# A decoder layer on one core: the front taken in pairs of tiles, half of the tokens first, with three loads issued from ScalarE's queue

## The chip, the core and the metric

One core of a Trainium2 chip runs the whole program. The time is the device time in microseconds (us) of one execution; lower is better. Three runs of the kernel before are at hand, and one further execution was recorded by the hardware profiler.

## The reference, cut to what matters

The layer takes x, 8 batches of 128 tokens with 512 features. The change is in its first stage, the mamba block up to the scores:

```python
h = rmsnorm(x, ln1_w)                 # x * rsqrt(mean(x * x) + eps) * ln1_w
zxbcdt = h @ w_in.T                   # 512 -> 1284: z, xs, Bs, Cs, dt
xBC = silu(conv4(xs | Bs | Cs) + conv_b)      # causal, 4 taps along the tokens, 768 channels
dt = softplus(dt + dt_bias)
cs = cumsum(dt * -exp(A_log))
att = (Cs @ Bs.T) * exp(cs_q - cs_k)          # for each batch and head
...
```

Behind it come the rest of the mamba block, a gated MLP, an attention over ctx and an expert layer, each with its normalisation. None of that is touched.

## The kernel before, in words

All products are made in three passes. An operand is split into a high part (rounded to the fp32r type) and a low part (the rest), and `three_pass` (L336) issues high x low, high x high and low x high; L338, L339 and L340 are these three matmuls. So each weight and each activation has to be split before TensorE may use it: ScalarE writes the high part by a copy (`hi_part` L653, `hi_of_hT` L685), and GpSimd (`lo_part` L281, the weights) or VectorE (`low1` L940, the activations) subtracts it for the low part.

**Tiles.** A tile is one batch of 128 tokens: x comes as eight tiles x0 to x7, and two halves (hf 0 and 1) of four tiles each make 512 columns. For each tile: ScalarE sums the squares (L665) and makes the reciprocal root by Ln and Exp (`rms`, L671 and L673), for two tiles at a time (`norm1(t0, t1)`); VectorE multiplies by it and by the LN1 row `ln1r`, which a DMA has broadcast to all 128 partitions (L931); TensorE turns the tile by four transposes (`turn_h`, L349) into bank 0 or 1; ScalarE and VectorE split what stands there (L687, L937).

**Weights.** `w_in` comes in six chunks of 128 x 1024 (0.5 MB), each of two blocks m of 128 output columns. A chunk is loaded into one of three raw buffers (`load_chunk`, L219), split by ScalarE (L657) and GpSimd (L283) into one of two ring buffers, and used by the projections of its two blocks. GpSimd counts `w_lo` when a chunk is ready; SyncE waits on it before it loads the next into the raw buffer, and ScalarE waits on `ip_done` before it writes the ring (`ring_hi`, L659).

**Projection.** Product n (`in_proj`, L352) is block m and half hf by `IN_ORDER` (L56): before, (0,0), (1,0), (0,1), (1,1), then m = 2 to 10 with both halves each. A whole product is 12 matmuls of 512 columns; in the front a product is also taken in two parts of 256 columns (two tiles). Products go round six banks (`IN_BANK`, L330), and a bank is free again when VectorE (`ip_used`) or ScalarE (`z_done`) has read it. Block 0 gives dt (`softplus_in`, L950; `softplus`, L689), blocks 1 to 6 go through the convolution (`conv_last_tap` L697 on ScalarE, three `conv_taps` L986 on VectorE, `conv_silu` L705 on ScalarE, with two buffers `acc`), blocks 7 to 10 are z. `time_steps` (L964) makes the cumulative sums, and `scores_of(0)` (L374) is issued after product 17; it needs those sums and the convolved values.

**Order.** Each engine has one instruction stream, written out by hand, and waits only on semaphores. TensorE's front is at L443 to L469: matmuls of zeros (`keep_warm`, L438) stand between the transposes and the first products. ScalarE's is at L742 to L765, VectorE's at L943 to L1003, GpSimd's at L285 to L295. SyncE issues all loads (L216 to L241), in this order: x0, x1, the LN1 row, x2, x3, chunk 0, eleven constants, x4 to x7, chunks 1 and 2, then the later chunks as they are waited for.

## Time and profile before

| what | us |
|---|---|
| median of 3 runs (lowest to highest) | 433.39 (433.07 to 433.83) |
| span of the profiled execution | 432.9 |
| that execution's own time, outside the span | not recorded; the median stands 0.5 above the span |
| TensorE busy in the span | 417.5 |
| VectorE / ScalarE / GpSimd busy | 211.8 / 161.4 / 67.6 |

The span runs from the first to the last instruction of the core. In the rows below, PE is TensorE's matmuls, PEld its weight loads, DVE VectorE, ACT ScalarE, POOL GpSimd and SP SyncE; a q behind a name is the engine's sequencer, which issues DMAs. A line number is that of the instruction in the kernel, which may be a helper's. Starts and ends of matmuls are modelled, so two that follow each other overlap in the rows: their pace is the distance of their starts.

### The profile page before, as it was taken

Reading aid. Unit: us, or ns where it says so; the run is one execution under the profiler, and the core shown is the slowest. Engines: PE = TensorE matmul, PEld = TensorE weight load, DVE = VectorE, ACT = ScalarE, POOL = GpSimd, SP = SyncE. Lnnn points to the kernel's source line nnn. Section 1 sums busy time; section 2 is a strip of 40 time slices with the busy share of each in tenths; the row PEclk is TensorE's granted clock in tenths of the full one; section 3 lists DMA queues with packets and bytes.
Section 4 is the critical chain, followed back from the end, with each engine's and each line's share of the span. In section 5 each row is a group of like instructions: output and inputs, shape, how many; then the busy total and the mean of one; then the engine's idle time right before and its main releaser. Section 6 shows DMA issues by size and latency. Waiting matters only on the chain.

```text
span 432.9 us, 5328 instructions
## 1 busy us (share of the span) xinstructions
PE 417.5 (96%) x1966; PEld 331.7 (77%) x1966; DVE 211.8 (49%) x392; ACT 161.4 (37%) x327; POOL 67.6 (16%) x51
## 2 busy tenths in 40 slices
PE   7999999999999999999999999999999999999984
PEld 2788887766667888888888888888787887887763
DVE  1586996135774431212122222254366576576566
ACT  5636655555653521212121212243232232241221
POOL 2412222344292110101010202020000000000000
PEclk9799999999999999999999999999999999999998
DMA  7610210020020021212121212111101201201001
GB/s 218 246 50 2 91 55 28 22 97 2 0 98 2 2 97 48 97 48 97 48 97 48 97 48 97 48 50 48 48 2 48 74 24 49 73 24 51 24 0 73
DMA packets 10256, 25.67 MB, mean 59 GB/s; under 512 B 1696, under 2 KB 1824, under 8 KB 10240
## 3 DMA queue, kind: packets, MB, share of 16 engines
q1 hardware_dynamic: 9088, 23.36, 16.1%
q10 hardware_dynamic: 1152, 2.10, 1.3%
q8 instruction: 10, 0.16, 0.2%
q14 instruction: 6, 0.05, 0.0%
HBM read 23.36 MB, written 2.10 MB: 59 GB/s over the span
## 4 chain that ended last, share of the span: by engine, by line
PE 88%; DVE 5%; ACT 3%; issue 1%; DMA 1%; SPq 0%; ACTq 0%; DVEq 0%
PE bank L338 25%; PE bank L339 25%; PE bank L340 25%; PE bank L394 2%; PE bank L382 2%; PE bank L546 2%; PE bank L535 1%; DMA rows<-x 1%; PE bank L557 1%; PE bank L403 1%; DVE tmp L1087 1%; PE bank L424 1%; PE bank L349 1%; PE bank L527 1%; PE bank L441 1%
## 5 line engine op out<-in xcount | busy, mean ns | idle before, releaser
L338 PE MATMUL bank<-cols,ringS 128*128 128x512 f32 (+1 forms) x328 | 126.6, 386 | 1.4 <-DVE cols L937 1.3
L340 PE MATMUL bank<-cols,ringS 128*128 128x512 f32 (+1 forms) x328 | 124.5, 380 | 0.0
L339 PE MATMUL bank<-cols,ringS 128*128 128x512 f32 (+1 forms) x328 | 124.5, 380 | 0.0
L338 PEld LDWEIGHTS bank<-cols,ringS 128*128 128x128 f32 x328 | 62.1, 189 | 15.0 <-issue 2.9
L339 PEld LDWEIGHTS bank<-cols,ringS 128*128 128x128 f32 x328 | 62.1, 189 | 11.8 <-issue 0.5
L340 PEld LDWEIGHTS bank<-cols,ringS 128*128 128x128 f32 x328 | 61.9, 189 | 11.6
L1054 DVE TENSOR_TENSOR big<-tmp,bank 128x512 f32 (+1 forms) x28 | 19.3, 688 | 102.2 <-ACT tmp L798 102.2
L338 PE MATMUL bank<-wdS,cols 128*128 128x512 f32 x144 | 61.4, 427 | 0.0
L340 PE MATMUL bank<-wdS,cols 128*128 128x512 f32 x144 | 56.4, 392 | 0.0
L339 PE MATMUL bank<-wdS,cols 128*128 128x512 f32 x144 | 56.2, 390 | 0.0
L798 ACT ACTIVATE tmp<-bank 128x512 f32<-128x512 f32 x28 | 16.8, 598 | 105.6 <-PE bank L340 105.6
L324 POOL TENSOR_TENSOR wdS<-raw,wdS 128x1024 f32 x7 | 16.8, 2394 | 122.2 <-ACT wdS L804 122.2
L338 PEld LDWEIGHTS bank<-wdS,cols 128*128 128x128 f32 x144 | 27.2, 189 | 7.7 <-issue 1.9
L339 PEld LDWEIGHTS bank<-wdS,cols 128*128 128x128 f32 x144 | 27.1, 189 | 6.6 <-issue 1.9
L340 PEld LDWEIGHTS bank<-wdS,cols 128*128 128x128 f32 x144 | 27.0, 188 | 6.0
L986 DVE SCALAR_TENSOR_TENSOR tmp<-bank,cw,tmp 128x508 f32<-128x508 f32 (+2 forms) x36 | 26.7, 742 | 5.5 <-ACT tmp L702 3.4
L283 POOL TENSOR_TENSOR ringS<-raw,ringS 128x1024 fp32r<-128x1024 f32 x8 | 20.2, 2533 | 52.8 <-ACT ringS L657 52.8
L837 ACT ACTIVATE small<-small 128x1 f32<-128x1 f32 x24 | 7.1, 294 | 50.7 <-DVE small L1089 50.7
L1059 DVE TENSOR_TENSOR ringS<-raw,ringS 128x1024 fp32r<-128x1024 f32 x14 | 17.2, 1227 | 2.3 <-ACT ringS L804 0.5
L1087 DVE BATCH_NORM_STATS2 tmp<-tmp 128x6 f32<-128x512 f32 x24 | 16.7, 694 | 0.8
L1009 DVE SCALAR_TENSOR_TENSOR big<-bank,xb,big 128x128 f32<-128x128 f32 x32 | 9.0, 342 | 16.5 <-ACT big L726 16.5
L937 DVE TENSOR_TENSOR cols<-bank,cols 128x512 fp32r<-128x512 f32 x16 | 10.9, 687 | 12.5 <-ACT cols L687 7.8
(134 smaller groups left out, 513.2 us busy)
## 6 DMA issues: line engine op xcount, KB each, us to landing
raw<-wstream SPq DMA_DIRECT2D x31, 512.0 KB, 3.2
rows<-x SPq DMA_DIRECT2D x8, 256.0 KB, 4.6
big<-ctxT SPq DMA_DIRECT2D x8, 256.0 KB, 2.6
big<-ctx SPq DMA_DIRECT2D x8, 256.0 KB, 2.9
out<-tmp ACTq DMA_DIRECT2D x8, 256.0 KB, 2.0
big<-ln_w SPq DMA_DIRECT2D x2, 256.0 KB, 5.4
big<-lora_b SPq DMA_DIRECT2D x3, 64.0 KB
ga<-gate_lora SPq DMA_DIRECT2D x1, 72.0 KB
```

The costliest lines, as they stand in the source:

```text
L283: pool.tensor_tensor(dst, raw[:, raw_slot(n), :], hi.bitcast(F32), ALU.subtract).then_inc(w_lo, 1)
L324: pool.tensor_tensor(wdS_t[:, bass.ds(j * CH + NM * D, CH)], raw[:, 0, :], wdS_t[:, bass.ds(j * CH, CH)].bitcast(F32), ALU.subtract).then_ ...
L338: pe.matmul(ps, a_hi, b_lo, start=first, stop=False)
L339: pe.matmul(ps, a_hi, b_hi, start=False, stop=False)
L340: return pe.matmul(ps, a_lo, b_hi, start=False, stop=last)
L798: act.activation(hn[:, par, :], bank[4 * par + 2 * hf][:, :], ACT.Silu).then_inc(sg_ok, 1)
L937: v.tensor_tensor(token_cols(t, 1), blocks(src), token_cols(t, 0).bitcast(F32), ALU.subtract).then_inc(done, 1)
L986: v.scalar_tensor_tensor(out=dst[:, :, s:L], in0=src[:, :, 0:L - s], scalar=cw[:, m, 3 - s:4 - s], in1=dst[:, :, s:L], op0=ALU.mult, op1=A ...
L1009: v.scalar_tensor_tensor(out=dec[:, b % 2, h, :], in0=bank[6][:, bass.ts(h, L)], scalar=xb[:, b % 2, P + H + h:P + H + h + 1], in1=dec[:, ...
L1054: v.tensor_tensor(dst, blocks(hn[:, par, :]), blocks(bank[4 * par + 2 * hf + 1][:, :]), ALU.mult) \
L1059: v.tensor_tensor(ringS[:, par, 1, :], raw[:, par + 1, :], ringS[:, par, 0, :].bitcast(F32), ALU.subtract).then_inc(ring_lo, 1)
L1087: v.bn_stats(stats[:, k, :], u).then_inc(ln_st[i], 1)
```

## The change

The front goes by pairs of tiles, and in the order of the products all four blocks of chunks 0 and 1 come first for half 0, then for half 1. Chunk 0 is loaded second, and it is split in two pieces with semaphores of their own (`w0_hi`, `w0_lo`). ScalarE's queue issues the LN1 row (one partition, 2 KB), x1 and chunk 1. The LN1 row is spread to 128 partitions by a matmul with ones into bank 7, and VectorE reads it there. The constants are two groups, four for the taps (`taps_in`) and seven others. `keep_warm` has 18 matmuls of zeros in place of 26, into bank 6. On ScalarE, softplus of half 1 moves behind the third convolution product. The core of the diff:

```diff
-IN_ORDER = ((0, 0), (1, 0), (0, 1), (1, 1)) + tuple((m, hf) for m in range(2, N_IN) for hf in range(2))
-N_CONST = 11
+IN_ORDER = tuple((m, hf) for hf in range(2) for m in range(4)) \
+    + tuple((m, hf) for m in range(4, N_IN) for hf in range(2))
+CONV_ORDER = tuple((m, hf) for m, hf in IN_ORDER if 1 <= m <= N_CONV)
+N_TAPS = 4
+N_CONST = 7
+def last_of_chunk(n):
+    return max(i for i, (m, hf) in enumerate(IN_ORDER) if m // 2 == n)
...
-        ln1r = big[:, 13312:13824]
+        ln1row = acc[0:1, 0, :]
+        LN1_BANK = 7
```

SyncE's loads:

```diff
-            for t in range(2):
-                sp.dma_start(rows[:, t, :], x[t]).then_inc(x_in[t], 16)
-            sp.dma_start(ln1r, ln1_w.partition_broadcast(P)).then_inc(ln1_in, 16)
-            for t in range(2, HB):
-                sp.dma_start(rows[:, t, :], x[t]).then_inc(x_in[t], 16)
+            load_rows(0, 1)
             load_chunk(0)
-            for dst, src in ((alog[:, :], a_log), (dtb[:, :], dt_bias), (cw[:, :, :], conv_w),
-                             (cb[:, :], conv_b), (dsk[:, :], d_skip.partition_broadcast(P)),
+            load_rows(2, HB)
+            load_rows(HB, HB + 2)
+            for dst, src in ((alog[:, :], a_log), (dtb[:, :], dt_bias), (cw[:, :, :], conv_w), (cb[:, :], conv_b)):
+                sp.dma_start(dst, src).then_inc(taps_in, 16)
+            load_rows(HB + 2, B)
+            load_chunk(2)
+            for dst, src in ((dsk[:, :], d_skip.partition_broadcast(P)),
                              (ln2r, ln2_w.partition_broadcast(P)), (ga[:, :, :], gate_lora),
                              *((lb[bass.ts(i, E * RANK), :], lora_b) for i in range(3)),
                              (eb[:, :], expert_bias.partition_broadcast(P))):
                 sp.dma_start(dst, src).then_inc(const_in, 16)
-            for t in range(HB, B):
-                sp.dma_start(rows[:, t, :], x[t]).then_inc(x_in[t], 16)
-            load_chunk(1)
-            load_chunk(2)
```

GpSimd's low parts of the weights:

```diff
-            for n in range(IN_CHUNKS):
+            for q in range(2):
+                q_ = bass.ts(q, D)
+                pool.wait_ge(w0_hi, q + 1)
+                pool.tensor_tensor(ringS[:, 0, 1, q_], raw[:, raw_slot(0), q_], ringS[:, 0, 0, q_].bitcast(F32),
+                                   ALU.subtract).then_inc(w0_lo, 1)
+            pool.wait_ge(w0_lo, 2)
+            pool.sem_inc(w_lo, 1)
+            for n in range(1, IN_CHUNKS):
                 lo_part(n, ringS[:, n % 2, 1, :], ringS[:, n % 2, 0, :])
-                if n == 0:
+                if n == 2:
```

TensorE's waits and its order up to n = 4:

```diff
-                pe.wait_ge(w_lo, m // 2 + 1)
+                if m < 2:
+                    pe.wait_ge(w0_lo, m + 1)
+                else:
+                    pe.wait_ge(w_lo, m // 2 + 1)
...
-            zeros = (7, idle[:, 0, 0:P], idle)
-            WARM = (4, 4, 2, 2, 2)
+            zeros = (6, idle[:, 0, 0:P], idle)
             pe.wait_ge(idle_ok, 1)
-            keep_warm(12, *zeros)
-            pe.wait_ge(pool_setup, 8)
+            keep_warm(10, *zeros)
+            pe.wait_ge(vec_setup, 1)
+            pe.wait_ge(ln1_in, 16)
+            pe.matmul(bank[LN1_BANK][:, :], ones[0:1, :], ln1row, start=True, stop=True).then_inc(ln1_ps, 1)
+            pe.wait_ge(pool_setup, 3)
             turn_h(0)
             turn_h(1)
-            keep_warm(WARM[0], *zeros)
+            keep_warm(4, *zeros)
+            in_proj(0, 2, 0)
+            in_proj(1, 2, 0)
+            keep_warm(2, *zeros)
             turn_h(2)
-            keep_warm(WARM[1], *zeros)
-            in_proj(0, 2, 0)
             turn_h(3)
-            in_proj(1, 2, 0)
-            keep_warm(WARM[2], *zeros)
+            keep_warm(2, *zeros)
             in_proj(0, 2, 1)
+            in_proj(1, 2, 1)
             turn_h(4)
-            in_proj(1, 2, 1)
             turn_h(5)
-            keep_warm(WARM[3], *zeros)
+            in_proj(2)
+            in_proj(3, 2, 0)
             turn_h(6)
-            in_proj(2, 2, 0)
             turn_h(7)
-            in_proj(3, 2, 0)
-            keep_warm(WARM[4], *zeros)
-            in_proj(2, 2, 1)
             in_proj(3, 2, 1)
```

ScalarE:

```diff
             def ring_hi(n):
                 if n >= 2:
-                    act.wait_ge(ip_done, 4 * (n - 1))
+                    act.wait_ge(ip_done, last_of_chunk(n - 2) + 1)
...
+            act.dma_start(ln1row, ln1_w.partition_broadcast(1)).then_inc(ln1_in, 16)
+            act.dma_start(rows[:, 1, :], x[1]).then_inc(x_in[1], 16)
+            act.dma_start(raw[:, raw_slot(1), :], wstream[1]).then_inc(raw_in[raw_slot(1)], 16)
             act.preload_act_table_set(LN_EXP)
             norm1(0, 2)
+            act.wait_ge(raw_in[raw_slot(0)], 16)
+            for q in range(2):
+                q_ = bass.ts(q, D)
+                act.activation(ringS[:, 0, 0, q_], raw[:, raw_slot(0), q_], ACT.Copy).then_inc(w0_hi, 1)
+            act.sem_inc(w_hi, 1)
+            hi_of_hT(0)
+            hi_of_hT(1)
             norm1(2, HB)
-            hi_of_hT(0)
-            hi_part(0, ringS[:, 0, 0, :])
-            hi_of_hT(1)
+            ring_hi(1)
             hi_of_hT(2)
+            hi_of_hT(3)
             norm1(HB, HB + 2)
-            hi_of_hT(3)
+            hi_of_hT(HB)
+            hi_of_hT(HB + 1)
             norm1(HB + 2, B)
-            ring_hi(1)
-            for t in range(HB, B):
-                hi_of_hT(t)
             conv_last_tap(0)
-            act.wait_ge(const_in, 16 * N_CONST)
+            hi_of_hT(HB + 2)
+            hi_of_hT(HB + 3)
             act.activation(expa[:, :], alog[:, :], ACT.Exp).then_inc(expa_ok, 1)
             softplus(0)
-            softplus(1)
             for i in range(1, 2 * N_CONV):
                 conv_last_tap(i)
+                if CONV_ORDER[i] == (1, 1):
+                    ring_hi(2)
+                    softplus(1)
                 conv_silu(i - 1)
-                if i % 4 == 1:
+                if i in (5, 9):
                     ring_hi(2 + i // 4)
```

VectorE:

```diff
-                    v.wait_ge(ln1_in, 16)
+                    v.wait_ge(ln1_ps, 1)
...
-                                       in1=ln1r, op0=ALU.mult, op1=ALU.mult).then_inc(hn1, 1)
+                                       in1=bank[LN1_BANK][:, :], op0=ALU.mult, op1=ALU.mult).then_inc(hn1, 1)
...
-            for t0 in (0, HB):
-                norm1(t0)
-                for t in range(t0 + 1, t0 + HB):
-                    norm1(t)
-                    low1(t - 1)
-                low1(t0 + HB - 1)
+            for t in range(0, B, 2):
+                norm1(t)
+                norm1(t + 1)
+                low1(t)
+                low1(t + 1)
...
             softplus_in(0)
-            conv_taps(0)
-            softplus_in(1)
-            conv_taps(1)
-            for i in range(2, 2 * N_CONV):
+            for i in range(2 * N_CONV):
+                if CONV_ORDER[i] == (1, 1):
+                    softplus_in(1)
                 conv_taps(i)
             time_steps(0)
             v.wait_ge(pool_setup, 8)
+            v.wait_ge(const_in, 16 * N_CONST)
```

## Rows read from the trace of the kernel before

**Rows 1.** Windows, whole core: stretch, length, busy us (instructions) by engine, clock, DMA share, GB/s.
```profile
0.00:31.50 31.50, 26.56 (x154) 19.54 (x155) 16.64 (x25) 17.16 (x39) 10.45 (x19) 0.89 0.54 176
31.50:70.00 38.50, 38.50 (x172) 31.47 (x170) 32.51 (x52) 23.07 (x34) 7.23 (x3) 1.00 0.13 42
```

**Rows 2.** Chain that ended last: start us, us, what.
```profile
2.19 5.65 DMA rows<-x
...
15.05 0.21 PE bank L339
...
22.35 1.76 DVE tmp L931
...
70.03 1.08 PE bank L382 x8
...
86.39 0.86 PE bank L403 x2
```

**Rows 3.** Timeline of the front: start us, us, engine line operation [idle before <- releaser].
```profile
1.30 5.02 PE L441 MATMUL bank<-big 128*128 128x512 bf16 x12 [1.30 <-DVE big L921]
...
4.42 0.63 ACT L665 ACTIVATE big<-rows 128x512 bf16<-128x512 f32 x1
...
5.64 0.20 ACT L673 ACTIVATE rst<-rst 128x2 f32<-128x2 f32 x1
...
7.24 1.41 DVE L931 SCALAR_TENSOR_TENSOR tmp<-rows,rst,big 128x512 f32<-128x512 f32 x2 [5.86 <-DMA big<-ln_w]
...
10.47 1.05 ACT L657 ACTIVATE ringS<-raw 128x1024 fp32r<-128x1024 f32 x1
...
11.61 2.56 POOL L283 TENSOR_TENSOR ringS<-raw,ringS 128x1024 fp32r<-128x1024 f32 x1 [7.48 <-ACT ringS L657]
...
12.65 2.07 DVE L931 SCALAR_TENSOR_TENSOR tmp<-rows,rst,big 128x512 f32<-128x512 f32 x1
...
14.27 0.78 PE L338 MATMUL bank<-cols,ringS 128*128 128x256 f32 x1
...
31.53 0.40 PE L338 MATMUL bank<-cols,ringS 128*128 128x512 f32 x1
```

**Rows 4.** Windows of the first 17 us, columns as in rows 1.
```profile
2.00:3.00 1.00, 1.00 (x4) 0.32 (x3) 0.00 (x0) 0.10 (x1) 1.00 (x2) 1.00 0.93 279
...
4.00:5.00 1.00, 1.00 (x4) 0.30 (x2) 0.00 (x0) 0.90 (x4) 0.13 (x4) 1.00 0.51 111
...
7.00:8.00 1.00, 0.00 (x0) 0.00 (x0) 0.76 (x2) 0.13 (x1) 0.00 (x0) 1.00 1.08 418
...
9.50:10.00 0.50, 0.50 (x3) 0.21 (x2) 0.00 (x0) 0.41 (x3) 0.00 (x0) 0.50 1.04 254
...
16.50:17.00 0.50, 0.50 (x7) 0.50 (x6) 0.00 (x0) 0.00 (x0) 0.04 (x1) 1.00 1.06 393
```

**Rows 5.** ScalarE's DMA issues: duration ns least/median/most, first and last start us.
```profile
L843 ACTq DMA_DIRECT2D out<-tmp x8: 338/342/397, 335.9 to 430.5; - x8
```

**Rows 6.** Groups by line and shape: count | busy us, mean ns | idle before.
```profile
L937 DVE TENSOR_TENSOR cols<-bank,cols 128x512 fp32r<-128x512 f32 x16 | 10.9, 687 | 12.5 <-ACT cols L687 7.8 <-ACT cols L740 4.4
```

**Rows 7.** Timelines of VectorE, ScalarE and GpSimd in the convolution stage.
```profile
28.21 0.73 DVE L957 TENSOR_SCALAR tmp<-bank,small 4x512 f32<-4x512 f32 x1
...
30.24 2.28 DVE L986 SCALAR_TENSOR_TENSOR tmp<-bank,cw,tmp 128x508 f32<-128x508 f32 x3
...
40.47 24.30 DVE L986 SCALAR_TENSOR_TENSOR tmp<-bank,cw,tmp 128x508 f32<-128x508 f32 x30 [1.26 <-ACT tmp L702]
...
31.01 0.72 ACT L695 ACTIVATE big<-big,small 4x512 f32<-4x512 f32 x1
...
36.89 1.28 ACT L709 ACT_TABLE_LOAD   x1
38.18 0.63 ACT L709 ACTIVATE big<-tmp 128x512 f32<-128x512 f32 x1
...
39.84 2.40 POOL L283 TENSOR_TENSOR ringS<-raw,ringS 128x1024 fp32r<-128x1024 f32 x1 [16.30 <-ACT ringS L657]
```

More of the change, by code:

```diff
@@ L152, in build @@
         gm = small[:, 15:17]
+        LN1_BANK = 7
         bank = [es.enter_context(nc.psum_tensor(f"bank{i}", [P, D], F32)) for i in range(8)]
         x_in = [sem(f"x_in{t}") for t in range(B)]
-        const_in = sem("const_in")
-        ln1_in = sem("ln1_in")
+        const_in, taps_in = sem("const_in"), sem("taps_in")
+        ln1_in, ln1_ps = sem("ln1_in"), sem("ln1_ps")
         raw_in = [sem(f"raw_in{i}") for i in range(RAW)]
@@ L168, in build @@
         w_hi = sem("w_hi")
+        w0_hi, w0_lo = sem("w0_hi"), sem("w0_lo")
         w_lo = sem("w_lo")
@@ L219, in load_chunk, with load_rows @@
                 sp.dma_start(raw[:, raw_slot(n), :], wstream[n]).then_inc(raw_in[raw_slot(n)], 16)
-            for t in range(2):
-                sp.dma_start(rows[:, t, :], x[t]).then_inc(x_in[t], 16)
-            sp.dma_start(ln1r, ln1_w.partition_broadcast(P)).then_inc(ln1_in, 16)
-            for t in range(2, HB):
-                sp.dma_start(rows[:, t, :], x[t]).then_inc(x_in[t], 16)
-            load_chunk(0)
-            for dst, src in ((alog[:, :], a_log), (dtb[:, :], dt_bias), (cw[:, :, :], conv_w),
-                             (cb[:, :], conv_b), (dsk[:, :], d_skip.partition_broadcast(P)),
+            def load_rows(t0, t1):
+                for t in range(t0, t1):
+                    sp.dma_start(rows[:, t, :], x[t]).then_inc(x_in[t], 16)
+            load_rows(0, 1)
+            load_chunk(0)
+            load_rows(2, HB)
[5 more added lines that the diff above has]
+            for dst, src in ((dsk[:, :], d_skip.partition_broadcast(P)),
                              (ln2r, ln2_w.partition_broadcast(P)), (ga[:, :, :], gate_lora),
@@ L332, in conv_product @@
         def conv_product(i):
-            return IN_ORDER.index((1 + i // 2, i % 2))
+            return IN_ORDER.index(CONV_ORDER[i])
         def three_pass(pe, ps, a_hi, a_lo, b_hi, b_lo, first, last):
@@ L379, in scores_of @@
                     pe.wait_ge(dec_exp, H * (b - 1))
+                if b == 0:
+                    pe.wait_ge(pool_setup, 8)
                 pe.matmul(bank[b % 2][:, :], identb[:, :], future, start=True, stop=False)
@@ L697, in conv_last_tap @@
             def conv_last_tap(i):
-                m, n = i // 2, conv_product(i)
+                m, n = CONV_ORDER[i][0] - 1, conv_product(i)
                 act.wait_ge(ip_done, n + 1)
+                if i == 0:
+                    act.wait_ge(taps_in, 16 * N_TAPS)
                 if i >= 2:
@@ L705, in conv_silu @@
             def conv_silu(i):
-                m, hf = i // 2, i % 2
+                m, hf = CONV_ORDER[i][0] - 1, CONV_ORDER[i][1]
                 act.wait_ge(cv_tap, 3 * (i + 1))
@@ L955, in softplus_in @@
                 if hf == 0:
-                    v.wait_ge(const_in, 16 * N_CONST)
+                    v.wait_ge(taps_in, 16 * N_TAPS)
                 v.tensor_scalar(dt_row[:, half(hf)], n_ps, dtb[:, 0:1], 0.0, ALU.add, ALU.max).then_inc(sp_step, 1)
@@ L977, in conv_taps @@
             def conv_taps(i):
-                m = i // 2
+                m = CONV_ORDER[i][0] - 1
                 src = bank[IN_BANK[conv_product(i)]][:, :].rearrange("p (b q) -> p b q", b=HB)
```

## The prediction

> **What bounds the kernel now.** The page's busy tenths come first: TensorE is the engine that is nearly always busy, but for the first slices. The windows then split the span: from 31.5 to 70 us it is busy the whole 38.50 us, while in the first 31.5 us it is busy 26.56 us at a mean granted clock of 0.89 [rows 1], and part of that is spent on zeros. So time can be won in the front only, and every microsecond by which the fifth projection product (n = 4, at 31.53) starts earlier moves all that follows, unless something behind it is late.
>
> The chain of waits says what holds the front: from 2.19 us on, 5.65 us for the third tile of x [rows 2]. The timeline has the details [rows 3]: squares of the second tile at 4.42, but the first normalised tile only at 7.24, after 5.86 us of idle time that the broadcast LN1 row ended; first weights split by ScalarE at 10.47, their low parts on GpSimd from 11.61 for 2.56; first product at 14.27. The windows of one microsecond show why the LN1 row is late: 111 GB/s in 4:5, when its broadcast is what the queue moves, against 418 in 7:8 [rows 4]. x2, x3 and the first weights stand behind it on SyncE's queue.
>
> **Pace.** A half-width matmul takes 0.21 us at 15.05 on the chain [rows 2]. A full-width one later takes 0.229 (168 of them, 14 products, from 31.53 to the scores at 70.03 [rows 2, 3]), a product 2.75, so half a width 0.12. The granted clock is 0.50 at 9.50 and 1.00 from 16.50 [rows 4], that is 1.2 and then 2.4 GHz. Before it fell, the engine had idled from 6.3 (12 matmuls of zeros, 5.02 us from 1.30) to 8.1.
>
> **Part 1, transfers.** ScalarE issues three DMAs first. Its issues in the tail take 0.34 each [rows 5], SyncE's at most 0.43: 1.0 to 1.3 us. The table load (1.28, as the one at 36.89 [rows 7]) then ends at 3.1 to 3.4 instead of 2.1, still ahead of x0, whose squares started at 3.60 (second squares at 4.42 [rows 3] less 0.82, 0.63 and the reading of the sum). Cost nothing; without that cover 1.3. The broadcast of 256 KB is gone for a row of 2 KB. x1 now shares the engines with the first weights: bounds 4.4 (as now) and 5.5 (512 KB, its own and as much of the weights, at the 279 GB/s of 2:3 [rows 4] after x0), taken 4.9, by the 418 GB/s of 7:8. The first weights need x0, x1, themselves and half of the second weights, about 1.3 MB, from 2.0 us on, and some 0.7 us to be seen (x0, moved at 279 GB/s, is whole at 2.9 and seen at 3.6): 5.9 at 418 GB/s, 7.4 at 279. I take 6.1, nearer to the first, since 7:8 is where weights move. On SyncE's queue x2 and x3 follow, half a MB, by 8.5: ScalarE wants them at 9.7. The four small taps, x6, x7, the third weights and the seven constants are issued behind; the first to be wanted is x4, at 16.6.
>
> The Trainium skill (DMA: Bandwidth & Descriptors, Issuing engines are not separate DMA queues) states that transfers from several engines run on the same DMA engines and interleave, and that only the issuing time is saved. By it the move to ScalarE's queue gives at most 3 x 0.43 us of issue, and the second weights, wanted at 11.9 only, are a load on the first. The interleaving is in the bounds above; it makes rival A.
>
> **Part 2, LN1 row by TensorE.** Ten matmuls of zeros end at 1.30 + 10 x 0.42 = 5.6. The outer product is one f32 matmul of 512 columns: 0.86 at the full clock [rows 2], 1.7 at half: 6.5 to 7.3. Taken 7.0. ScalarE has the scales at 4.9 + 1.4 = 6.3 (from the second squares at 4.42 to the end of rms at 5.84 [rows 3]; a pair is 2.2). So the first normalise starts at 7.05, near the 7.24 of now. VectorE then reads one operand from PSUM. Two of the eight L931 take 2.07 and 1.75, each beside GpSimd's subtract (the first at 12.65 under the one from 11.61 [rows 2, 3]), and the others about 0.7. L937, which reads a bank, keeps a mean of 0.687 over all 16 [rows 6], those beside GpSimd among them. I give the new L931 0.75 throughout. Of the two long ones the second is on the chain: 1.0 us won.
>
> **Part 3, weights first.** From 6.35 ScalarE splits the first weights in two halves of 0.55 (1.05 for both [rows 3]). GpSimd follows each with 1.28 (half of 2.56 [rows 3]): ready at 8.2 and 9.5. Tiles 0 and 1: normalised 7.05 to 8.4, turned by 9.0, high parts (0.6 each) to 9.65, low parts (0.69 each) to 10.4. The tiles end last, and the first product starts at **10.45** against 14.27.
>
> **Part 4, the new order up to n = 4.** Two half products are 24 matmuls: 2.85 us at full clock, 5.1 at half. Nearest row: half, from 9.5 on. But TensorE idles under a microsecond at a time now, so I take 12 at half and 12 at full: to 14.4. Zeros 0.45. ScalarE squares tiles 2 and 3 from 9.65 to 11.85, splits the second weights until 12.9 (GpSimd to 15.5). Their normalise ends at 13.3; turned 14.9 to 15.9, high to 16.55, low to 17.3. Half products of these tiles 17.35 to 20.2. Tiles 4 and 5: squares from 16.55, normalised by 20.15, turned by 21.2. Product 2 and half of 3 from there, 2.75 + 1.43, to 25.4; in their shade squares 6 and 7 until 24.05, normalise until 25.45. Turned by 26.4; last half 26.4 to 27.85, with low(7) done at 27.75. So n = 4 starts at **27.85**, 3.7 before 31.53. With full clock throughout, the same steps give 26.7. The 8 fewer matmuls of zeros (18 for 26) are inside these times.
>
> **Part 5, what is late next.** The low parts of tile 7 release VectorE's convolution. softplus_in takes 2.03, the first taps 2.28, ScalarE's Ln ends 3.5 after softplus_in starts (28.21, 30.24, 31.01 + 0.72 [rows 7]). From 27.75: last_tap(1) 31.9, table load and silu(0) 33.8, last_tap(2) 34.5, silu(1) 35.1, last_tap(3) 35.8. Only behind it stands ring_hi(2), the third weights: 1.05 to 36.8, GpSimd 2.40 to 39.3 [rows 7]. TensorE wants them at 27.85 + 4 x 2.75 = 38.85. A new stall of **0.5**. In the old kernel they were ready at 39.84 + 2.40 = 42.24, for 42.5.
>
> Then softplus(1) stands between silu(1) and silu(2): two table loads more, 2.56. Exp waits for VectorE (38.75): Ln to 40.2, load to 41.5, silu(2) 42.1, last_tap(4) 42.8. VectorE idles 1.7, then keeps 2.43 a product (24.30 for ten [rows 7]): conv(9) done at 57.3, and TensorE needs its bank at 39.3 + 7 x 2.75 = 58.5. Last conv 62.1, first scan 63.7, scores at 66.8. The fourth weights, behind silu(4), are ready at 49.2 for 50.3. The cover is 1.1 us in the weights and 1.2 in the bank: the loads cost nothing while it holds, and 1.3 more of delay (if the Exp's load is made only after its wait) would show as 0.3.
>
> The Trainium skill (ScalarE: Activation LUTs, What ACT_TABLE_LOAD costs) gives a switch 2.66 us with its drain. No row here shows that drain: the load takes 1.28 and is followed at 38.18 by silu [rows 7]. By the page's figure the two switches would be an estimated 2.8 later, and rival C comes of it.
>
> **The sum.** 3.7 - 0.5 = 3.2 us. The profiled span of 432.9 becomes 429.7; the median of the runs, 433.39, stands 0.5 above the span, so **430.2**.
>
> **Rivals.**
> A, the transfers hold the start: x1 at 5.5, first weights at 7.4 or later. ScalarE's splits then stand ahead of its high parts of tiles 0 and 1, and 1 to 1.5 us is lost: about 431.5. For it: 1.3 MB in one go. Against: ScalarE is busy to 6.3 anyway. Chance 0.15.
> B, it ends slower: TensorE's clock stays at 1.2 GHz through the front. 84 more half-width equivalents at 0.09 cost 7.6, less 1.0 of idle time: 3.4 slower, 436.8. The gain is gone after some 45 of them, at about 24 us. For it: fewer zeros, and TensorE waits for tiles at 14 to 17. Against: from 10.45 on it has more work than from 12 to 16.2, after which the clock rose. Chance 0.07.
> C, the convolution takes it back: each table switch 2.7 instead of 1.3. silu(4) and so the fourth weights are 2.8 later, 1.7 of it uncovered: 431.9. Against: the row of the load. Chance 0.07.
> D, no change: another wait in the front, such as tiles 2 and 3 behind ScalarE's splits, leaves n = 4 within a microsecond of now: 433. Chance 0.06.
> E, full clock throughout and LN1 at 6.5: n = 4 at 26.4: 428.8. Chance 0.15.
> The forecast has 0.5.
>
> **The numbers.** The forecast's own range is 429.2 to 431.2. With E below and A and C above: 428.6 to 432.0, about 0.15 outside. A measurement of this kernel tells 0.2%, 0.87 us. Faster 0.87 (forecast, A, C, E), same 0.06 (D), slower 0.07 (B).
>
> **What would show it.** First half product near 10.5, with the granted clock beside it; no L931 over 0.8; tile 0 no longer waiting for a broadcast; n = 4 (first 128x512 of L338) at 26.5 to 28; a wait of about 0.5 for GpSimd ahead of n = 8; four table loads before the scores instead of two; scores at 66 to 67; from there to the end the same distance as now. It is wrong if n = 4 comes after 30, if the clock is at 0.5 beyond 16 us, or if TensorE waits for weights or banks for over a microsecond between n = 4 and the scores.

## The result, and the profile after

The kernel became slower by 0.3%. Over ten runs of each its median is 434.78 us (433.71 to 436.04) against 433.50 us (432.88 to 434.41) before: ratio 1.0032, 95% interval 1.0021 to 1.0044. A later measurement (e5) gave 434.49 against 433.75: 1.0020 (1.0006 to 1.0034). Forecast were 430.2 us and a range of 428.6 to 432.0.

The page of the changed kernel: its head and its busy shares.

```profile
span 432.6 us, 5302 instructions
PE 415.1 (96%) x1948; PEld 329.8 (76%) x1948; DVE 212.5 (49%) x392; ACT 165.0 (38%) x331; POOL 67.5 (16%) x52
```

The profiled execution took 434.83 us, 2.2 more than its span. TensorE is still busy nearly all the time, so the change must be sought in when its work starts. Windows of the changed kernel (stretch, length, busy us with the number of instructions for TensorE, its weight loads, VectorE, ScalarE and GpSimd, granted clock, DMA share, GB/s), first the two stages that answer to [rows 1], then pieces of the front that answer to [rows 4]:

```profile
0.00:28.60 28.60, 23.48 (x136) 17.71 (x137) 11.47 (x21) 15.90 (x38) 8.10 (x18) 0.94 0.54 185
28.60:69.65 41.05, 39.21 (x170) 31.32 (x170) 34.97 (x53) 27.89 (x38) 9.50 (x5) 1.00 0.12 39
...
4.00:5.00 1.00, 1.00 (x5) 0.23 (x2) 0.00 (x0) 0.37 (x2) 0.13 (x4) 1.00 0.98 381
...
9.50:10.00 0.50, 0.50 (x4) 0.50 (x3) 0.00 (x0) 0.50 (x1) 0.50 (x1) 0.50 1.05 369
```

Two things stand here. The front is 2.9 us shorter than in [rows 1] (28.60 for 31.53), with 381 and 369 GB/s where [rows 4] had 111 and 254. But the stage from n = 4 to the scores, 38.50 us long and wholly busy in [rows 1], is now 41.05 long, of which TensorE is busy only 39.21. Most of the front's gain was given back behind it. What is left by these two executions, 0.3 us in favour of the change, is not what the runs say; why is shown with e9.

The timeline of the front of the changed kernel (start us, us, engine, line, operation, idle time before and who ended it), which answers to [rows 3]:

```profile
0.82 0.54 ACTq L767 DMA_DIRECT2D tmp<-ln_w  x1
1.39 0.37 ACTq L768 DMA_DIRECT2D rows<-x  x1
1.79 0.44 ACTq L769 DMA_DIRECT2D raw<-wstream  x1
2.26 1.28 ACT L770 ACT_TABLE_LOAD   x1 [2.26 <-issue]
...
5.03 1.12 PE L473 MATMUL bank<-tmp,ones 1*128 1x512 f32 x2
...
6.00 0.63 ACT L688 ACTIVATE big<-rows 128x512 bf16<-128x512 f32 x1 [1.63 <-DMA rows<-x]
...
7.33 1.13 ACT L775 ACTIVATE ringS<-raw 128x512 fp32r<-128x512 f32 x2
7.46 1.41 DVE L966 SCALAR_TENSOR_TENSOR tmp<-rows,rst,bank 128x512 f32<-128x512 f32 x2 [6.08 <-ACT rst L696]
...
11.80 0.35 PE L357 MATMUL bank<-cols,ringS 128*128 128x256 f32 x1 [0.16 <-DVE cols L972]
...
17.89 0.36 PE L357 MATMUL bank<-cols,ringS 128*128 128x256 f32 x1 [1.23 <-DVE cols L972]
...
28.60 0.47 PE L357 MATMUL bank<-cols,ringS 128*128 128x512 f32 x1 [0.24 <-DVE cols L972]
```

The second tile of x is squared at 6.00 after a wait of 1.63 us for its transfer; before, with x1 second on SyncE's queue, it was at 4.42 [rows 3]. VectorE's first normalise no longer waits for the row of LN1 (which the outer product at 5.03 delivers) but for ScalarE's scales, which x1 holds back; it starts at 7.46, no earlier than the 7.24 of [rows 3]. The first product starts at 11.80 for 14.27.

The convolution stage of the changed kernel, in the same columns, which answers to [rows 7]:

```profile
30.51 0.63 ACT L716 ACTIVATE big<-big 4x512 f32<-4x512 f32 x1 [2.82 <-DVE big L994]
31.18 0.72 ACT L718 ACTIVATE big<-big,small 4x512 f32<-4x512 f32 x1
...
37.74 1.28 ACT L716 ACT_TABLE_LOAD   x1
37.80 2.39 POOL L295 TENSOR_TENSOR ringS<-raw,ringS 128x1024 fp32r<-128x1024 f32 x1 [21.37 <-ACT ringS L680]
39.29 1.44 DVE L994 SCALAR_TENSOR_TENSOR big<-big 4x512 f32<-4x512 f32 x1
40.24 0.19 PEld L357 LDWEIGHTS bank<-cols,ringS 128*128 128x128 f32 x1 [0.94 <-POOL ringS L295]
40.24 0.50 PE L357 MATMUL bank<-cols,ringS 128*128 128x512 f32 x1 [0.52 <-POOL ringS L295]
40.76 0.63 ACT L716 ACTIVATE big<-big 4x512 f32<-4x512 f32 x1 [1.74 <-DVE big L994]
41.41 1.28 ACT L718 ACT_TABLE_LOAD   x1
42.71 0.72 ACT L718 ACTIVATE big<-big,small 4x512 f32<-4x512 f32 x1
43.45 1.28 ACT L734 ACT_TABLE_LOAD   x1
...
50.34 2.38 POOL L295 TENSOR_TENSOR ringS<-raw,ringS 128x1024 fp32r<-128x1024 f32 x1 [7.76 <-ACT ringS L680]
...
52.78 0.19 PEld L357 LDWEIGHTS bank<-cols,ringS 128*128 128x128 f32 x1 [1.74 <-POOL ringS L295]
52.78 0.50 PE L357 MATMUL bank<-cols,ringS 128*128 128x512 f32 x1 [1.32 <-POOL ringS L295]
```

Here are the 2.6 us that the stage gained in length (41.05 less the 38.45 that the old order takes in e1; 38.50 in [rows 1]). TensorE waits twice for low parts of weights from GpSimd: for the third chunk at 40.24 and for the fourth at 52.78. Its weight loads stood still 0.94 and 1.74 us, 2.7 together; the matmuls' own idle time, 0.52 and 1.32, shows less. Ahead of the second wait ScalarE makes **three** table loads around softplus(1), at 37.74 for Exp, 41.41 for Ln and 43.45 for silu. Two were forecast. In softplus(0), at 30.51 and 31.18, Ln follows Exp without a load, under the table that the kernel had loaded by name at 2.26; behind a silu each of the two gets a load of its own.

### The profile page after: what moved, and what is told of

Read it like the earlier page. It is cut to its first block, busy times and chain, and to the rows that moved or that the text cites. A ratio compares the mean times of both kernels' runs of the same rounds, so it can differ in the third digit from the quotient of the medians.

```text
span 432.6 us, 5302 instructions
## 1 busy us (share of the span) xinstructions
PE 415.1 (96%) x1948; PEld 329.8 (76%) x1948; DVE 212.5 (49%) x392; ACT 165.0 (38%) x331; POOL 67.5 (16%) x52
## 4 chain that ended last, share of the span: by engine, by line
PE 83%; DVE 8%; ACT 5%; issue 1%; DMA 1%; POOL 1%; ACTq 0%; DVEq 0%; POOLq 0%
PE bank L357 23%; PE bank L359 23%; PE bank L358 23%; PE bank L418 2%; PE bank L406 2%; PE bank L569 2%; PE bank L558 1%; DVE cols L972 1%; PE bank L580 1%; DMA rows<-x 1%; DVE tmp L1020 1%; PE bank L427 1%; PE bank L368 1%; DVE tmp L1121 1%; PE bank L448 1%
## 5 line engine op out<-in xcount | busy, mean ns | idle before, releaser
L357 PEld LDWEIGHTS bank<-cols,ringS 128*128 128x128 f32 x324 | 60.9, 188 | 19.7 <-issue 5.4
L358 PEld LDWEIGHTS bank<-cols,ringS 128*128 128x128 f32 x324 | 60.9, 188 | 12.0 <-issue 0.5
L359 PEld LDWEIGHTS bank<-cols,ringS 128*128 128x128 f32 x324 | 60.9, 188 | 11.8
L295 POOL TENSOR_TENSOR ringS<-raw,ringS 128x1024 fp32r<-128x1024 f32 x7 | 17.7, 2529 | 48.7 <-ACT ringS L680 48.7
L1128 DVE TENSOR_SCALAR tmp<-tmp,small 128x512 f32<-128x512 f32 x24 | 12.9, 538 | 7.6 <-ACT small L874 7.6
```

What stands on the lines that cost most here:

```text
L295: pool.tensor_tensor(dst, raw[:, raw_slot(n), :], hi.bitcast(F32), ALU.subtract).then_inc(w_lo, 1)
L357: pe.matmul(ps, a_hi, b_lo, start=first, stop=False)
L358: pe.matmul(ps, a_hi, b_hi, start=False, stop=False)
L359: return pe.matmul(ps, a_lo, b_hi, start=False, stop=last)
L1128: v.tensor_scalar(u, u, mv[:, k, 0:1], lrs[:, k:k + 1], ALU.subtract, ALU.mult).then_inc(ln_out[i], 1)
```

## The experiments

Theory 1 says what the two traces show: the loss is in the weights' producers behind n = 4 (softplus(1) with its table loads, and ring_hi(2) behind last_tap(3)), and the front gained less than it seems. Its rivals put the loss outside the span (three transfers issued by ScalarE), in the transfers (x1 beside the weights), or in TensorE's clock. The expectations number the theories in their own way; each says what its numbers mean.

All experiments with the times of the kernel before on the same chip (e1 to e4 on one, e5 to e8 on a second, e9 and e10 on a third, e11 and e12 later on the second). The ratios are computed over all the runs and are not quite the quotients of the medians; t0 is the first product, n4 the start of n = 4, sc the start of the scores, from each one's profiled execution:

| run | us | before, us | ratio (95%) | t0 | n4 | sc | n4 to sc |
|---|---|---|---|---|---|---|---|
| e1 before, x1 from ScalarE | 433.53 | 433.74 | 0.9995 (0.9986 to 1.0003) | 13.93 | 30.27 | 68.72 | 38.45 |
| e2 after, all from SyncE | 433.88 | as e1 | 1.0005 (0.9990 to 1.0019) | 10.89 | 27.68 | 68.65 | 40.97 |
| e3 after, one table for Exp and Ln | 433.28 | as e1 | 0.9986 (0.9973 to 0.9998) | 11.25 | 28.52 | 68.28 | 39.76 |
| e4 after, softplus(1) late | 433.05 | as e1 | 0.9994 (0.9981 to 1.0008) | 10.85 | 28.25 | 67.56 | 39.31 |
| e5 after again | 434.49 | 433.75 | 1.0020 (1.0006 to 1.0034) | 11.39 | 28.19 | 69.16 | 40.97 |
| e6 e4, third weights earlier | 431.92 | as e5 | 0.9960 (0.9948 to 0.9973) | 11.01 | 28.04 | 66.52 | 38.48 |
| e7 e6, x1 alone on SyncE | 431.68 | as e5 | 0.9959 (0.9943 to 0.9975) | 10.77 | 27.55 | 66.06 | 38.51 |
| e8 e7, 4 more zeros | 431.05 | as e5 | 0.9946 (0.9931 to 0.9962) | 10.30 | 27.09 | 65.59 | 38.50 |
| e9 before again (one execution) | 433.67 | | | 14.03 | 30.37 | 68.83 | 38.46 |
| e10 before, LN1 row by TensorE | 432.45 | 434.08 | 0.9971 (0.9955 to 0.9986) | 12.46 | 28.50 | 66.97 | 38.47 |
| e11 e10, 4 more zeros | 432.27 | 433.69 | 0.9977 (0.9964 to 0.9990) | 12.06 | 28.02 | 66.45 | 38.43 |
| e12 e8 again | 430.82 | as e11 | 0.9932 (0.9919 to 0.9946) | 12.79 | 29.98 | 68.47 | 38.49 |

**e1: of the old kernel, x1 alone issued from ScalarE.**

```diff
-            for t in range(2):
+            for t in range(1):
                 sp.dma_start(rows[:, t, :], x[t]).then_inc(x_in[t], 16)
...
+            act.dma_start(rows[:, 1, :], x[1]).then_inc(x_in[1], 16)
```

> The kernel before with one edit: x1 is issued from ScalarE's queue. Of the changed kernel, time less span is 2.2 us in every run (434.83 - 432.6, 436.04 - 433.8); of the kernel before it is about 0.6 (433.5 - 432.9). Theory 1, a first use of ScalarE's queue at the start adds the 1.6 outside the span: time less span 2.2 here, and 1 to 1.7 us slower than before. Rival, the 1.6 come from something else in the change (more semaphores, other memory): time less span stays 0.6, and the time is within 0.5 us of before.

Nothing came of it that can be measured, neither gain nor loss, and its time stands 2.07 us above its span, as the kernel before does in the runs beside it (2.06). So one transfer from ScalarE costs nothing outside the span. These runs also gave spans of the kernel before: over 35 of them the median is 431.7 (430.5 to 433.8), and the profiled execution of the prediction, at 432.9, was one of the long ones.

**e2: the changed kernel with all transfers on SyncE's queue.**

```diff
             load_rows(0, 1)
+            sp.dma_start(ln1row, ln1_w.partition_broadcast(1)).then_inc(ln1_in, 16)
+            load_rows(1, 2)
             load_chunk(0)
             load_rows(2, HB)
+            load_chunk(1)
...
-            act.dma_start(ln1row, ln1_w.partition_broadcast(1)).then_inc(ln1_in, 16)
-            act.dma_start(rows[:, 1, :], x[1]).then_inc(x_in[1], 16)
-            act.dma_start(raw[:, raw_slot(1), :], wstream[1]).then_inc(raw_in[raw_slot(1)], 16)
```

> The changed kernel with the three loads back on SyncE's queue (x0, LN1 row, x1, first weights, x2, x3, second weights, then as before). Theory 1: time less span falls from 2.2 to 0.6, and the time to about 433.1, unless the front starts later; second squares by 5 instead of 6.0, so n = 4 at 27.8 to 28.6. Rival (the queue has no cost outside the span): time less span stays 2.2, the time 434 to 435.

From n = 4 to the scores it is as long as in the changed kernel, 40.97 us, so ScalarE's queue has no part in that loss. The x1 squares hardly moved (timeline of e2):

```profile
5.68 0.63 ACT L691 ACTIVATE big<-rows 128x512 bf16<-128x512 f32 x1 [1.31 <-DMA rows<-x]
```

Time less span is 1.97, for 2.2 in every run with the three issues on ScalarE: this is what they cost outside the span, 0.2 us. The ratio, 1.0005, is also lower than the changed kernel's 1.0020 and 1.0032, but the intervals overlap, and where e6 and e7 make most of the same move on one chip, no more than those 0.2 us come of it.

**e3: the table that holds both Exp and Ln loaded by name ahead of softplus(1).**

```diff
+                    act.preload_act_table_set(LN_EXP)
                     softplus(1)
```

> The changed kernel with a load of the table that holds both Exp and Ln ahead of softplus(1), so that two tables are loaded there and not three. Theory 2, the third load is on the path that sets the fourth weights: silu(2) 1.3 earlier, the wait of TensorE for the fourth weights (1.3 us at 52.8) falls to about 0, and the span is 1.2 shorter (431.4). Rival, VectorE or a bank sets it: the wait moves to another releaser and the span is less than 0.5 shorter.

Timeline of e3, ScalarE and the two weight loads:

```profile
37.64 1.28 ACT L796 ACT_TABLE_LOAD   x1
40.15 0.19 PEld L357 LDWEIGHTS bank<-cols,ringS 128*128 128x128 f32 x1 [0.90 <-POOL ringS L295]
40.67 0.63 ACT L716 ACTIVATE big<-big 4x512 f32<-4x512 f32 x1 [1.74 <-DVE big L995]
41.33 0.73 ACT L718 ACTIVATE big<-big,small 4x512 f32<-4x512 f32 x1
42.08 1.28 ACT L734 ACT_TABLE_LOAD   x1
...
51.43 0.19 PEld L357 LDWEIGHTS bank<-cols,ringS 128*128 128x128 f32 x1 [0.53 <-POOL ringS L295]
```

Ln follows Exp at once, one load of 1.28 is gone, and the wait for the fourth weights falls from 1.74 to 0.53. The stage is 1.2 to 1.3 us shorter, 39.76. The wait was expected to fall to about nothing and does not; with softplus(1) gone altogether, in e4, it is gone. The wait for the third weights (0.90) stays, as it should: it comes before the softplus.

**e4: softplus(1) and its time steps moved behind the convolution.**

```diff
-                    softplus(1)
...
+            softplus(1)
...
-            time_steps(1)
+            time_steps(1)
```

> The changed kernel with softplus of half 1 moved between decay(0) and decay(1), where its table is loaded anyway, and its sums behind att(0) on VectorE: no table load more than in the kernel before. Theory 2: the wait for the fourth weights is gone, as in e3 (1.3 us), VectorE's convolution ends 3 to 4 us earlier than at 65.8, the wait for the third weights (0.5) stays: span 431.3. Rival, the late sums delay att(1) or the scores: a new wait for VectorE at 80 us and the gain is given back.

VectorE then keeps its taps in one unbroken group, and a single wait is left (timeline of e4):

```profile
39.88 0.19 PEld L357 LDWEIGHTS bank<-cols,ringS 128*128 128x128 f32 x1 [0.92 <-POOL ringS L295]
40.31 21.85 DVE L1020 SCALAR_TENSOR_TENSOR tmp<-bank,cw,tmp 128x508 f32<-128x508 f32 x27
```

The stage is 39.31, 0.86 over the old 38.45: the 0.92 of that wait. In the times e4 cannot be told from the kernel before (0.9994) nor from e3; its gain of 0.45 over e3 is seen in the traces only.

**e5: the changed kernel again, unaltered, on the chip of e6 to e8.**

> The changed kernel itself, on one chip with the three that follow and with the kernel before. Theory 3, the profiled execution of before was one of its slow ones for the clock (span 432.9 where the median of 35 is 431.7): the changed kernel is at a median span of 432.5 again, 0.5 to 1 us over before, and its executions fall in groups some 1.2 us apart by the clock at the start. Rival, the two kernels differ only by the chip they ran on: within 0.3 us of before here.

It repeats: slower, 1.0020; n = 4 at 28.19; 40.97 from there to the scores; time less span 2.18.

**e6: e4 with ring_hi(2) ahead of ScalarE's second silu of the new order.**

```diff
-                if CONV_ORDER[i] == (1, 1):
+                if i == 2:
                     ring_hi(2)
```

> e4 with the third weights split one convolution product earlier on ScalarE (ahead of silu(1), not behind last_tap(3)). Theory: they are ready at 38.5 where TensorE wants them at 39.3, so the wait of 0.5 is gone and n = 4 to the scores takes 38.5, as in the kernel before: span 0.5 below e4's 430.6 to 430.8. Rival: the convolution is delayed by 1.05 and the wait comes back at the fourth weights or a bank; no gain.

No wait for GpSimd is left between n = 4 and the scores; the stage is 38.48, as in the old kernel, and the time 0.9960. With e3 and e4 this accounts for the 2.6 us, by one trace each and in this order of steps: 1.3 for the third table load, 0.45 for the rest of softplus(1), 0.85 for ring_hi(2) behind last_tap(3). That the three together are worth that much the times show too: 1.0020 for the changed kernel, 0.9960 here, on one chip.

**e7: e6 with x0 and x1 ahead of everything on SyncE, second weights behind x3, and ScalarE issuing the LN1 row only.**

```diff
-            load_rows(0, 1)
+            load_rows(0, 2)
             load_chunk(0)
             load_rows(2, HB)
+            load_chunk(1)
...
-            act.dma_start(rows[:, 1, :], x[1]).then_inc(x_in[1], 16)
-            act.dma_start(raw[:, raw_slot(1), :], wstream[1]).then_inc(raw_in[raw_slot(1)], 16)
```

> e6 with x1 second on SyncE's queue, the first weights behind it, the second weights behind x3, and only the LN1 row on ScalarE's queue. Theory 4, x1 was late (second squares at 6.0, 5.6 at best) because it shared the transfer with the weights: second squares at 4.4 to 4.9, first half product 1 us earlier unless the first weights are then late (they would be seen by 6.9), span 0.5 to 1 us below e6. Rival: the weights come later by as much as x1 comes earlier, and the first product does not move.

x1 is squared at 4.49 for 5.47 in e6, but the first weights now hold ScalarE, which waits 1.10 us and splits them at 7.01 for 6.80. n = 4 came 0.5 earlier in the profiled execution, but the two ratios, 0.9960 and 0.9959, are one: nothing that can be measured.

**e8: e7 with four more matmuls of zeros behind the LN1 product**, and **e12**, the same kernel once more.

```diff
+            keep_warm(4, *zeros)
             pe.wait_ge(pool_setup, 3)
```

> e7 with four more matmuls of zeros between the LN1 product and the first transposes, where TensorE idles for 1.2 to 2.2 us ahead of the fall of the clock at 8 to 9 us. Theory 3: the clock stays at 2.4 GHz (1.00 from 8 to 12 us), the executions lie closer together, and the median is 0.5 to 1 us lower. Rival: the zeros delay the transposes by more than they give back; the same or slower.

> e8 again, on the same chip as e11: a median span of 429.0 and a ratio to before of 0.9946 if the first result holds; the comparison with e11 is the purpose.

The ratio of e8, 0.9946, has an interval that overlaps e7's; with e12's 0.9932 this version beats both kernels. The zeros' own share stays unproven. Timeline of e8, where x1 is squared early and the first weights end the wait on ScalarE:

```profile
4.52 0.63 ACT L690 ACTIVATE big<-rows 128x512 bf16<-128x512 f32 x1
...
6.87 1.15 ACT L775 ACTIVATE ringS<-raw 128x512 fp32r<-128x512 f32 x2 [0.93 <-DMA raw<-wstream]
```

The profiled execution of e12 is another matter: the same kernel, yet n = 4 comes 2.9 us later than in e8. A window and the timeline of e12 (columns as above):

```profile
9.50:10.00 0.50, 0.50 (x4) 0.50 (x3) 0.00 (x0) 0.00 (x0) 0.50 (x2) 1.00 1.13 310
...
5.68 2.07 PE L474 MATMUL bank<-tmp,ones 1*128 1x512 f32 x2
...
13.13 0.42 PE L359 MATMUL bank<-cols,ringS 128*128 128x256 f32 x1
13.35 0.42 PE L360 MATMUL bank<-cols,ringS 128*128 128x256 f32 x1
...
13.74 0.28 PE L359 MATMUL bank<-cols,ringS 128*128 128x256 f32 x1
13.86 0.28 PE L360 MATMUL bank<-cols,ringS 128*128 128x256 f32 x1
```

The record gives the clock as 1.00 in every window of the front, but the LN1 product takes 2.07 for the 1.12 of the changed kernel, and half-width matmuls follow each other every 0.22 us up to 13.57 and every 0.12 after: the engine went at 1.2 GHz till then. It starts so in the kernel before too, where the twelve matmuls of zeros at 1.30 take 5.02 us, 0.42 each [rows 3], under a clock of 1.00 [rows 4]; but in e8 the LN1 product, at 5.45, already takes 1.12. So in e12 the first rise of the clock came some 8 us later than in e8. This execution is the longest of e12's seven, with a span of 431.5 where the other six have 428.4 to 429.2, and e8's was one of the short ones (428.5, median 429.0). Executions of one kernel thus lie up to 3 us apart by the moment at which the clock rises. Why it rises earlier in one than in another was not found.

**e9: the kernel before again, one profiled execution.**

> The kernel before, profiled once more. Theory 3: an execution near the median span of 431.7 has n = 4 at 30.2 to 30.6, not at 31.53 as in the execution that the prediction was made from, and from there 38.4 to the scores, as there. If this execution too has its clock at 0.50 from 9.5 to 16, n = 4 is again at 31.5 and nothing is told apart. Rival: n = 4 is at 31.5 with the clock at 1.00.

A window and the timeline of e9:

```profile
9.50:10.00 0.50, 0.50 (x3) 0.09 (x1) 0.00 (x0) 0.41 (x3) 0.00 (x0) 1.00 1.18 359
...
7.67 0.63 ACT L665 ACTIVATE big<-rows 128x512 bf16<-128x512 f32 x1 [1.79 <-DMA rows<-x]
...
12.45 2.08 DVE L931 SCALAR_TENSOR_TENSOR tmp<-rows,rst,big 128x512 f32<-128x512 f32 x1
...
14.03 0.39 PE L338 MATMUL bank<-cols,ringS 128*128 128x256 f32 x1 [0.69 <-POOL ringS L283]
...
15.56 0.60 PE L349 MATMUL bank<-ident,tmp 128*128 128x128 f32 x4
...
30.37 0.40 PE L338 MATMUL bank<-cols,ringS 128*128 128x512 f32 x1
```

The transposes behind the first twelve half-width matmuls, in the execution of the prediction:

```profile
16.73 0.60 PE L349 MATMUL bank<-ident,tmp 128*128 128x128 f32 x4
```

The first product of e9 starts at 14.03, near the 14.27 of [rows 3], but n = 4 at 30.37, 1.2 us before the 31.53 there. The granted clock reads 1.00 where [rows 4] has 0.50, and since e12 shows that this record can be wrong, the pace has to bear it out. It does: the first twelve matmuls take 1.53 us here (14.03 to 15.56) and 2.46 there (14.27 to 16.73). These 0.93 and the 0.24 of the start are the 1.2 us. Against this execution, whose span of 431.8 is the ordinary one, the changed kernel's front is 1.8 to 2.2 us ahead, not 2.9.

**e10: of the change, the LN1 row alone**: the old kernel with a 2 KB row on one partition, ten zeros and one outer product for twelve zeros, and the normalise reading the bank. **e11** adds four matmuls of zeros behind the product.

```diff
-            sp.dma_start(ln1r, ln1_w.partition_broadcast(P)).then_inc(ln1_in, 16)
+            sp.dma_start(ln1row, ln1_w.partition_broadcast(1)).then_inc(ln1_in, 16)
...
-            keep_warm(12, *zeros)
+            keep_warm(10, *zeros)
+            pe.matmul(bank[7][:, :], ones[0:1, :], ln1row, start=True, stop=True).then_inc(ln1_ps, 1)
...
-                                       in1=ln1r, op0=ALU.mult, op1=ALU.mult).then_inc(hn1, 1)
+                                       in1=bank[7][:, :], op0=ALU.mult, op1=ALU.mult).then_inc(hn1, 1)
```

> The kernel before with the LN1 row alone changed: 2 KB to one partition in its old place in the queue, a matmul with ones into bank 7, and VectorE reading it there (ten matmuls of zeros ahead of it, not twelve, into bank 6). By the prediction's part 2 the first normalise moves little and the 1.0 of the chain at 22.35 (GpSimd beside VectorE with two operands in SBUF) is gone, and the transfers behind the broadcast come earlier: n = 4 at about 29, 1 to 1.5 us faster. Rival: the chain goes round it (ScalarE and the order of the tiles set the pace) and under 0.5 us is won.

> e10 (the old order, the LN1 row alone changed) with four more matmuls of zeros between the LN1 product and the first transposes, as in e8. If the new order gives something of its own once its table loads and waits are mended, e8 is over 0.5 us faster than this on the same chip (e8's median span was 429.0, e10's 430.5). Rival, the order gives nothing and e8's lead over e10 is the zeros: this has a span of about 429.0 to 429.5 too.

Timeline of e10:

```profile
5.66 0.61 ACT L668 ACTIVATE big<-rows 128x512 bf16<-128x512 f32 x1
...
11.04 0.74 DVE L934 SCALAR_TENSOR_TENSOR tmp<-rows,rst,bank 128x512 f32<-128x512 f32 x1
...
28.50 0.40 PE L338 MATMUL bank<-cols,ringS 128*128 128x512 f32 x1
```

With the old order of products, n = 4 is at 28.50, where the whole change has it at 28.60 and 28.19, and the time is 0.9971 of the old one. But this execution is one of the short ones of e10 (span 429.9, median 430.5); behind n = 4 all executions of it take the same, so n = 4 of an ordinary one stands near 29.1, an estimate from these three numbers. The medians of the spans are the safer measure: 430.5 for 432.05 before on that chip, 1.5 us won. x2 is there at 5.66 instead of 7.67 (the broadcast no longer holds the queue), and no normalise takes over 0.75, the one at 11.04 in spite of a subtract on GpSimd from 10.00 to 12.36. Four zeros more (e11, 0.9977) changed nothing that can be measured; e11's spans are 1.5 us below those of before as well (430.2 for 431.7).

## Why the prediction was wrong

The miss is 434.8 less 430.2, 4.6 us, and it has three places, by the profiled executions: n = 4 at 28.60 for 27.85 (0.75); 2.6 us lost between n = 4 and the scores for 0.5 (2.1); and 2.2 us outside the span for 0.5 (1.7). From the scores to the end both kernels take the same, 362.9, as forecast.

**The sum's base failed.** "The median of the runs, 433.39, stands 0.5 above the span" joined a long execution to an ordinary median. Time less span has a median of 2.0 in the later runs of that kernel, and its spans have a median of 431.7 (e1, e5, e11), so the span on which the sum rested was 1.2 us above the ordinary one, and its own time was presumably near 435, which was not recorded. Those 1.2 us lay in the front, in the half-speed matmuls of [rows 2, 4], as e9 shows, and the forecast booked them as a gain of the change (31.53 to 27.85). Of the 1.7 these are 1.2; 0.3 is that the median of three runs, 433.39, lay below the 433.7 of the later ones; and 0.2 is the cost of ScalarE's issues outside the span. Span 432.9 for a median time of 433.39 would have been worth one question: is that the execution which the median stands for?

**Part 1** was off at its main term. x1 beside the weights was seen at 6.00 (forecast 4.9, bounds 4.4 and 5.5; 5.68 in e2, 5.47 in e6). The first weights did not hold ScalarE, which split them from 7.33 without a wait. The three issues (0.54, 0.37 and 0.44) moved the table load's end to 3.54, forecast at most 3.4, at no cost. Rival A described this start well and priced it at 1 to 1.5 us; n = 4 lost 0.75, or 0.3 in e5. "ScalarE is busy to 6.3 anyway" spoke against it, but ScalarE was idle, waiting for x1. The Trainium skill (DMA: Bandwidth & Descriptors, Issuing engines are not separate DMA queues) states that transfers from several engines interleave and that only issuing time is saved. The traces agree: e1's move gave nothing, and x1 beside the weights comes at 6.00 from ScalarE's queue and at 5.68 from SyncE's.

**Part 2** was right, and it was most of the gain. The first normalise came at 7.46 (7.05), and what was said of the long normalises holds. Group of the changed kernel (line, operation, count, busy us, mean ns, idle time):

```profile
L966 DVE SCALAR_TENSOR_TENSOR tmp<-rows,rst,bank 128x512 f32<-128x512 f32 x8 | 5.6, 744 | 10.1 <-ACT rst L696 10.1
```

The same group in e9, which reads the broadcast row from SBUF:

```profile
L931 DVE SCALAR_TENSOR_TENSOR tmp<-rows,rst,big 128x512 f32<-128x512 f32 x8 | 8.1, 1036 | 5.7 <-DMA big<-ln_w 5.7
```

2.5 us less of VectorE's time over eight instructions, with 0.75 forecast for each. What was not seen is that the removed broadcast also brings x2 forward by two microseconds. By the medians of the spans e10 and e11 win 1.5 us without any new order, where the prediction gave this part 1.0; how the 1.5 divide between the shorter normalises and the earlier x2 no run shows. The whole change, in e5, has a span 0.6 longer than before (432.3 for 431.7) with 2.5 lost behind n = 4, so its front won 1.9.

**Parts 3 and 4** were half right. The first product came at 11.80, 11.39 in e5 (10.45), held by x1 and then by the tiles; the first 24 matmuls went at full clock from the start (11.80 to 14.75), better than the twelve at half of the forecast. Tiles 2 and 3 at 17.89 for 17.35. But the new order as it stood, with its loads and its split of the first weights, added little to the row's gain: 1.9 for 1.5, and 0.4 between measurements made at different times is not clear of noise. It starts products earlier and then waits 1.23 us for tiles. That it can pay was shown only with its faults mended: e12 against e11, both with four more zeros and on one chip, is 430.82 to 432.27, 1.5 us.

**Part 5** named the right places and mis-sized both. The third weights: wait forecast 0.5, found 0.52 at the matmuls but 0.94 at the weight loads, and 0.83 in the length of the stage (e4 to e6). The fourth weights: "two table loads more, 2.56", of which "the loads cost nothing", was the step that turned the sign. There are three; Exp and Ln used one table in the prediction because the old kernel has no load between them, but there the table was the one that the kernel had loaded by name, as it still is in softplus(0) at 30.51, and behind a silu a load stands ahead of each. softplus_in took 2.87 us (37.86 to 40.73) for the forecast's 2.03, its last step 1.44 beside GpSimd for 0.68 at 29.79. So the fourth weights were ready at 52.72, 2.8 later than the forecast's 49.2 moved by the 0.75 of n = 4; the cover of 1.1 us was used up and 1.74 were waited. The text had a bound for it ("1.3 more of delay ... would show as 0.3") but only with a load after its wait, not with a load more.

**The rivals.** C, "the convolution takes it back", had the right place and mechanism class at 0.07, though through a further load and not through dearer ones: each took 1.28, with the activation right behind (41.41 and 42.71). The Trainium skill (ScalarE: Activation LUTs, What ACT_TABLE_LOAD costs) gives a switch 2.66 us with its drain; these rows do not show it: a load is 1.28, and taking one out shortened the stage by 1.2 to 1.3 (e3). B, a clock that stays low, did not come; E's full clock did in part. D's time, 433, was nearest to the measured one, by luck: its mechanism, an n = 4 left where it was, did not come. The sentence on what would prove it wrong, that TensorE waits for weights for over a microsecond between n = 4 and the scores, came true, and there were five table loads before the scores for the four that were forecast.

By corrected terms the sum is: 1.8 to 2.2 won in the front, 2.6 lost behind it, 0.2 outside the span: 0.6 to 1.0 slower; measured 1.3 and 0.7.

## What to carry to other kernels

Before a sum is made against one profiled execution, compare its span and clock with the median of the runs: a long execution's slow stretch is booked as gain by any change near it. When work is moved between other functions on ScalarE, count a table load for every function whose table is not the one loaded just before, and load a table that holds them all by name. When the consumer starts earlier, follow every in-order producer behind it (here the splits of weights behind last taps and a softplus) before the gain is counted; and take a change apart by its parts first, since here one part carried most of the gain and the others cost more than they brought.

## What the runs showed of the hardware

- The profile's granted clock can be 1.00 while matmuls go at half pace: e12 has, before the first rise, an outer product of 2.07 for 1.12 and half-width matmuls every 0.22 us under a clock of 1.00. Take the pace from the matmuls.
- One kernel's executions differ by up to 3 us in the front by the moment at which the clock rises (n = 4 at 27.09 in e8, 29.98 in e12); the mean clock of the record does not rank them (0.996 and 0.998).
- A broadcast of one 2 KB row to 128 partitions holds what is queued behind it: 111 GB/s while it moves [rows 4], and x2 two microseconds later (7.67 for 5.66).
- VectorE's pass with two operands in SBUF takes up to 2.08 beside GpSimd (12.45 in e9), and 0.74 beside it with one of them in PSUM (11.04 in e10).
- Idle time of the weight loads measures what a late weight costs better than that of the matmuls: 0.94 and 1.74 for 0.52 and 1.32, where 2.6 us were lost.
- Three transfers issued by ScalarE at the start cost 0.2 us outside the span (time less span 2.2 for 2.0), one costs nothing (e1, 2.07).
